# Turning the normalised tokens of an attention and expert layer: eight TensorE turns a group, or VectorE turns of 32 x 32 squares with SBUF exchanges

## What is computed

```python
# first layer, on layernorm(x)
g = jax.nn.sigmoid(jnp.einsum('bld,ed->ble', x, Wg) + bg)
h[l] = (1 - g[l]) * h[l-1] + g[l] * x[l]          # associative scan over l
attn = jnp.einsum('bld,ed->ble', h, Wo) + bo
x = x + layernorm(attn)
# second layer, on layernorm(x), E = 8 experts, C = 320, H = 1024
probs = jax.nn.softmax(xf @ router_w + router_b); eid = argmax(probs)
rank = position of the token among those of its expert; valid = rank < C
y_tok = relu(x @ w1[eid] + b1[eid]) @ w2[eid] + b2[eid]      # where valid
yov   = relu(xf @ ow1 + ob1) @ ow2 + ob2                      # otherwise
x = x + layernorm(where(valid, y_tok, yov))
```

## Time and profile before

| | us |
|---|---|
| median of 3 runs | 1164.59 (1164.39 to 1166.16) |
| the profiled execution | 1166.17 |
| its span in the profile | 1163.0 |

### The profile page before, as it was taken

The page is one execution under the profiler, slowest core; times in us unless marked ns, Lnnn a source line. Parts: engine busy times, 40 slices in busy tenths (PEclk is TensorE's granted clock), DMA queues, the critical chain, the costliest instruction groups (busy, mean ns, idle before and its releaser), DMA issues.

```text
span 1163.0 us, 24424 instructions
## 1 busy us (share of the span) xinstructions
PE 1142.6 (98%) x7549; PEld 1020.4 (88%) x7549; DVE 991.5 (85%) x2741; ACT 742.1 (64%) x1375; POOL 690.1 (59%) x792
## 2 busy tenths in 40 slices
PE   8999999999999999999999999999999999999996
PEld 4788898888988898888888888988898888899996
DVE  6888988888888988989898888888888987688885
ACT  4366666666656666666666666656666666678782
POOL 3556567675656666565657665656666664414444
PEclk9999999999999999999999999999999999999998
DMA  9121110100111111111101101111111100335430
GB/s 262 58 100 56 55 46 35 43 27 30 36 36 36 36 36 36 36 36 36 36 19 35 34 23 33 36 36 36 36 36 36 36 18 20 114 114 191 145 130 34
DMA packets 59428, 65.09 MB, mean 56 GB/s; under 512 B 7835, under 2 KB 55629, under 8 KB 59268
## 3 DMA queue, kind: packets, MB, share of 16 engines
q1 hardware_dynamic: 52228, 59.36, 15.8%
q0 software_dynamic: 7168, 5.34, 1.5%
HBM read 40.19 MB, written 38.76 MB: 68 GB/s over the span
## 4 chain that ended last, share of the span: by engine, by line
PE 90%; DVE 5%; POOL 2%; ACT 1%; issue 1%; DMA 0%; DVEq 0%; POOLq 0%; ACTq 0%
PE psY L1430 12%; PE psY L1433 11%; PE psY L1432 11%; PE psH L1324 11%; PE psH L1325 11%; PE psH L1326 10%; PE psA L1324 5%; PE psA L1325 5%; PE psA L1326 5%; PE psT L1380 3%; PE psT L1337 2%; DVE st L859 1%; PE psT L1393 1%; PE psT L1395 1%; PE psA L1498 1%
## 5 line engine op out<-in xcount | busy, mean ns | idle before, releaser
L621 ACT ACTIVATE hid<-psH,biasT 128x512 f32<-128x512 f32 (+1 forms) x312 | 202.9, 650 | 217.6 <-PE psH L1326 215.2
L1430 PE MATMUL psY<-W_hi,hid_hi 128*128 128x256 f32 x1168 | 336.1, 288 | 0.6 <-DVE hid_lo L1012 0.5
L1433 PE MATMUL psY<-W_hi,hid_lo 128*128 128x256 f32 x1168 | 330.3, 283 | 0.0
L1432 PE MATMUL psY<-W_lo,hid_hi 128*128 128x256 f32 x1168 | 330.2, 283 | 0.0
L399 POOL TENSOR_TENSOR rstd<-veps,mhalf 128x4 f32<-128x4 f32 (+2 forms) x103 | 141.4, 1373 | 163.2 <-DVE nmean L871 163.2
L1012 DVE TENSOR_TENSOR hid_lo<-hid,hid_hi 128x512 fp32r<-128x512 f32 (+1 forms) x308 | 200.6, 663 | 42.5 <-ACT hid_hi L626 35.8
L1324 PE MATMUL psH<-xfT_hi,W_hi 128*128 128x512 f32 (+1 forms) x624 | 235.9, 378 | 0.3 <-ACT hid L621 0.2
L1325 PE MATMUL psH<-xfT_lo,W_hi 128*128 128x512 f32 (+1 forms) x624 | 234.9, 376 | 0.0
L1326 PE MATMUL psH<-xfT_hi,W_lo 128*128 128x512 f32 (+1 forms) x624 | 232.7, 373 | 0.0
L1430 PEld LDWEIGHTS psY<-W_hi,hid_hi 128*128 128x128 f32 x1168 | 222.7, 191 | 9.9 <-DVE hid_lo L1012 1.6
L1432 PEld LDWEIGHTS psY<-W_lo,hid_hi 128*128 128x128 f32 x1168 | 223.0, 191 | 5.9
(11 more groups left out here) (173 smaller groups left out, 2176.8 us busy)
## 6 DMA issues: line engine op xcount, KB each, us to landing
xin<-L_attn_x SPq DMA_DIRECT2D x32, 512.0 KB, 3.4
stage<-L_ffn_w SPq DMA_DIRECT2D x16, 1024.0 KB, 5.2
out<-outt SPq DMA_DIRECT2D x31, 512.0 KB, 2.8
xbuf<-zrow SPq DMA_DIRECT2D x1, 2590.0 KB, 16.5
xin<-xbuf SPq DMA_DIRECT2D x8, 259.0 KB, 4.9
stage<-L_ffn_ow SPq DMA_DIRECT2D x2, 1024.0 KB, 8.5
xbuf<-x,idx POOLq DMA_INDIRECT x128, 2.1
b_b<-L_ffn_b SPq DMA_DIRECT2D x1, 1024.0 KB, 6.5
```

The lines of the kernel that those rows point to most:

```text
L621: act.activation(hid[j % 2][:, at:n], psH[:, j % 2, at:n], ACT.Relu, bias=bias).then_inc(s_hid, 1)
L1430: pe.matmul(dst, hi, w[0][:, j, :], start=(j == 0 and (tail or t % 2 == 0)), stop=False, skip_group_check=True)
L1432: pe.matmul(dst, hi, w[1][:, j, :], start=False, stop=False, skip_group_check=True)
L1433: last = pe.matmul(dst, lo_, w[0][:, j, :], start=False, stop=(j == HC - 1), skip_group_check=True)
```

## The change

From group 6 on (`PIPED`) the tokens are turned without TensorE. For such a group:

- x is loaded a second time, a step earlier, into `x_ahead`, the first half of stage (`load_ahead`); statistics and norm0 read it there. xin is still loaded for residual1.
- VectorE's stats0 handles group g+4 instead of g+3, as one piece ahead of lo(7); before, the moments stood behind xf_lo.
- GpSimd's norm0 handles g+3 instead of g+2, in the same place of the step. Before it writes tok it waits until the blocks of the group before have landed.
- SP exchanges tok into `tok_blocks[v]` (the second half of stage) with 16 DMAs of 32 partitions each, SBUF to SBUF, behind the load of x (`exchange_blocks`). A DMA moves the square (b, a) of each 128x128 tile to (a, b), in runs of 32 elements (128 bytes).
- VectorE turns each 32 x 32 square of tok_blocks into psT with two `transpose` instructions of 128x512, between stats1 and residual2 (`turn_blocks`).
- TensorE leaves out transposes0 in those steps (26 of them).
- The first expert's weights are loaded in the steps 28 and 29 instead of step 1, since stage is in use until then. Steps 2 and 3 are written out instead of looped, and the last four steps of GpSimd.

The diff, cut to its core:

```diff
+SQ = 32
+PIPED = 6
...
+def piped(g):
+    return not isinstance(g[0], int) or 2 * g[0] + g[1] >= PIPED
...
+        tok_blocks = [stage[:, 1, v * TG * D:(v + 1) * TG * D].rearrange("p (t d) -> p t d", d=D) for v in range(2)]
+        x_ahead = stage[:, 0, 0:TG * D].rearrange("p (t d) -> p t d", d=D)
+
+        def xin_of(g):
+            return x_ahead if piped(g) else xin[g[1]]
...
+            def load_ahead(g):
+                i, v = g
+                if piped(grp(i, v, -1)):
+                    sp.wait_ge(s_tok, cnt(g, 1, 0))
+                sp.sem_inc(s_held_sp, 1)
+                sp.dma_start(x_ahead, x[i, v * GT:(v + 1) * GT, :].rearrange("(t p) d -> p t d", p=P))\
+                    .then_inc(s_x_ahead[v], 16)
+
+            def exchange_blocks(g):
+
+                i, v = g
+                src = tok[:].rearrange("p t d -> p (t d)").rearrange("p (n c) -> p n c", c=P)
+                dst = tok_blocks[v].rearrange("p t d -> p (t d)").rearrange("p (n c) -> p n c", c=P)
+                sp.wait_ge(s_tok, cnt(g, 1, 1))
+                sp.sem_inc(s_held_sp, 1)
+                sp.wait_ge(s_T0, cnt(grp(i, v, -1), 2, 0))
+                sp.sem_inc(s_held_sp, 1)
+                for a in range(P // SQ):
+                    for b in range(P // SQ):
+                        sp.dma_start(dst[a * SQ:(a + 1) * SQ, :, b * SQ:(b + 1) * SQ],
+                                     src[b * SQ:(b + 1) * SQ, :, a * SQ:(a + 1) * SQ]).then_inc(s_blocks[v], 16)
...
-                prev, nxt, far = grp(i, u, -1), grp(i, u, 1), grp(i, u, 3)
+                prev, nxt, far, beyond = grp(i, u, -1), grp(i, u, 1), grp(i, u, 3), grp(i, u, 4)
+                if piped(beyond) and live(beyond, NG):
+                    load_ahead(beyond)
                 if live(prev, NG):
                     store(prev)
                 if live(far, NG):
                     sp.wait_ge(s_x1, cnt(nxt, 1, 1))
                     load(far)
+                    if piped(far):
+                        exchange_blocks(far)
...
-                pool.wait_ge(s_T0, cnt(g, 2, 0))
+                before = grp(i, v, -1)
+                if piped(before):
+                    pool.wait_ge(s_blocks[before[1]], landed((before[0] - PIPED // 2, before[1]), (P // SQ) ** 2))
+                else:
+                    pool.wait_ge(s_T0, cnt(g, 2, 0))
                 pool.sem_inc(s_held, 1)
                 for t in range(TG):
-                    last = pool.tensor_scalar(tok[:, t, :], xin[v][:, t, :], rstd[0][:, t:t + 1], nmr[0][:, t:t + 1],
+                    last = pool.tensor_scalar(tok[:, t, :], xin_of(g)[:, t, :], rstd[0][:, t:t + 1], nmr[0][:, t:t + 1],
...
-                if live(far, NG):
+                if not piped(far):
                     norm0(far)
+                elif live(beyond, NG):
+                    norm0(beyond)
                 if live(nxt, NG):
                     deviation(1, nxt, TG)
+                    if piped(beyond) and not piped(far):
+                        norm0(beyond)
...
+            def turn_blocks(g):
+                i, v = g
+                dve.wait_ge(s_blocks[v], landed((i - PIPED // 2, v), (P // SQ) ** 2))
+                for c in range(DC):
+                    dve.transpose(psT[:, c, :], tok_blocks[v][:, :, c * P:(c + 1) * P]).then_inc(s_T0, 1)
...
+                if piped(grp(i, u, 3)) and not piped(far):
+                    stats0(grp(i, u, 3))
...
                     stats1(nxt)
+                if ahead and piped(far):
+                    turn_blocks(far)
                 if live(grp(i, u, -1), NG):
                     residual2(grp(i, u, -1))
...
-                next_x = grp(i, u, 3)
+                next_x = grp(i, u, 4 if piped(grp(i, u, 3)) else 3)
                 if live(next_x, NG):
-                    read_rows0(next_x)
+                    stats0(next_x)
                 low(7)
                 if up:
                     xf_lo(nxt, GT)
-                if live(next_x, NG):
-                    moments(0, next_x, TG)
...
-                    if j == 3 and ahead:
+                    if j == 3 and ahead and not piped(far):
                         transposes0(far)
```

More of the change, by code:

```diff
@@ L210, in sandwich_kernel @@
         s_T0 = sem("s_T0")
+        s_blocks = sems("s_blocks")
+        s_x_ahead = sems("s_x_ahead")
+        s_held_sp = sem("s_held_sp")
         s_xn_hi = sem("s_xn_hi")
@@ L327, in _ @@
             sp.wait_ge(s_l2, HC)
-            load_w1((0, 0))
-            load_w2((0, 0))
             step(0, 1)
-            with sp.Fori(1, NG // 2 - 2) as i:
+            for u in range(2):
+                step(1, u)
+            with sp.Fori(2, NG // 2 - 2) as i:
                 for u in range(2):
                     step(i, u)
-            for u in range(4):
-                step(*grp(NG // 2 - 2, u, 0))
+            step(NG // 2 - 2, 0)
+            sp.wait_ge(s_tok, NG)
+            load_w1((0, 0))
+            step(NG // 2 - 2, 1)
+            sp.wait_ge(s_T0, 2 * NG)
+            load_w2((0, 0))
+            for u in range(2):
+                step(NG // 2 - 1, u)
             def load_rows(e):
@@ L465, in step @@
                 prev, now, nxt, far = grp(i, u, -1), grp(i, u, 0), grp(i, u, 1), grp(i, u, 2)
+                beyond = grp(i, u, 3)
                 if live(prev, NG):
                     deviation(3, prev, TG, t0=sure(prev))
-                if live(far, NG):
+                if not piped(far):
                     norm0(far)
+                elif live(beyond, NG):
+                    norm0(beyond)
                 if live(nxt, NG):
                     deviation(1, nxt, TG)
+                    if piped(beyond) and not piped(far):
+                        norm0(beyond)
                     renumber(nxt)
@@ L515, in _ @@
             second_step((0, 0), (0, 1), (1, 0), (1, 1))
-            with pool.Fori(1, NG // 2 - 1) as i:
+            for u in range(2):
+                step(1, u)
+            with pool.Fori(2, NG // 2 - 2) as i:
                 for u in range(2):
                     step(i, u)
-            for u in range(2):
-                step(NG // 2 - 1, u)
+            for u in range(4):
+                step(*grp(NG // 2 - 2, u, 0))
             def keep_rows(e):
@@ L880, in read_rows0 @@
                 i, v = g
-                dve.wait_ge(s_x_in[v], landed(g))
-                read_rows(0, lambda t: xin[v][:, t, :], TG)
+                if piped(g):
+                    dve.wait_ge(s_x_ahead[v], landed((i - PIPED // 2, v)))
+                else:
+                    dve.wait_ge(s_x_in[v], landed(g))
+                read_rows(0, lambda t: xin_of(g)[:, t, :], TG)
             def stats0(g):
@@ L1252, in _ @@
             second_step(*(grp(0, 0, k) for k in range(5)))
-            with dve.Fori(1, NG // 2 - 2) as i:
+            for u in range(2):
+                step(1, u)
+            with dve.Fori(2, NG // 2 - 2) as i:
                 for u in range(2):
@@ L1595, in _ @@
             second_step(A, B, (1, 0), (1, 1))
-            with pe.Fori(1, NG // 2 - 1) as i:
+            for u in range(2):
+                step(1, u)
+            with pe.Fori(2, NG // 2 - 1) as i:
                 for u in range(2):
```

## The result

In its first measurement the changed kernel takes **1188.5 us** (median of 4 runs, 1187.6 to 1189.2), the kernel before 1164.5 (1164.2 to 1166.2): ratio 1.0199, 95% interval 1.0186 to 1.0212. It is 24 us slower where 3.9 us less were forecast, and 0.5 us above the range. The profiled execution took 1188.88 us, 1187.1 of them span. The same kernel, not a character changed, took 1181.7 us in a second measurement and **1159.7 us** in a third (e13, ratio 0.9952, 0.9936 to 0.9969), while the medians of the kernel before lay between 1164.3 and 1165.4 in every measurement.

A forecast was written before the change was run, and what follows sets the result against it. TensorE, busy 98%, was taken to set a 31.17 us step; VectorE's and GpSimd's loops would then limit it to 31.02, saving 26 x 0.15 = 3.9 us from 1164.59, giving 1160.7 us. The range was 1150 to 1188.

The forecast's parts named there:

- VectorE starts its result as soon as layer2(7) ends, so this closes a loop: At the step's end: lo(7) delayed to 29.42, next step starts at 31.00 us, so VectorE paces the step.
- 0.26 us late already: Before layer2(2): VectorE's lo(2) ends at 14.16 us of the step, where TensorE, 0.90 early, wants it at 13.90.
- limits of 31.00 and 31.04 us: Step lengths set by VectorE's loop and by GpSimd's through tok2; they fall together, and 31.02 was taken.
- The turn: Between stats1 and residual2 on VectorE: two 128x512 transposes at 0.70 us each, 1.40 for both.
- The fourth rival: On VectorE: the turn costs as much as the scan, 2.42 us; step 32.0, +22 us, 1187 us. Chance 15%.
- The estimate from the Trainium skill's figure: For VectorE's 128x512 turn: 0.73 us, from the skill's 311 ns for a 128x128 bf16 turn.
- TensorE's matmuls: At transposes0 (L1337): 26 x 8 = 208 matmuls go, 0.90 us a step less on TensorE.
- GpSimd's loop: From stats2's nmean: tok2 at 27.23 us makes transposes1 wait, step 31.04; hst_lo at 34.91 makes project 0.4 late.
- VectorE's loop: Turn 1.40 and moments 0.68 us, less idle time, put lo(7) at 29.42; the step is 31.00 us.
- Full gain: The turn hides in VectorE's spare time, so TensorE's 26 x 0.90 = 23 us come whole: 1141 us. Chance 7%.
- Held moments: Moments ahead of lo(7) caught behind a GpSimd instruction: 0.5 us a step, +9 us, 1173 us. Chance 26%.
- Late blocks: Exchanged blocks land after GpSimd's norm0 needs them, 38.6 us after step start: 1180 up to 1300 us. Chance 8%.

The follow-up runs named there:

- e13: The changed kernel once more, unaltered, in its third measurement: 1159.7 us, ratio 0.9952 to the kernel before.
- session A: The first measurement of the changed kernel, beside the kernel before (a session is kernels measured together on one chip, one after the other): 1188.5 us.
- e8: The kernel before with one line moved: the moments of the next x ahead of lo(7) instead of behind xf_lo. 1164.1 us, ratio 0.9997.
- e11: The changed kernel with neither exchange nor turn on VectorE: TensorE transposes again, moments still ahead of lo(7); a repeat of e2, unaltered. 1165.8 us.
- e10: The changed kernel without the 16 exchange transfers: GpSimd writes into the block buffers, VectorE turns the unexchanged squares, values wrong. 1164.9 us here, 1160.1 us when first measured.
- e9: The changed kernel once more, unaltered, in its second measurement: 1181.7 us.
- e17: The changed kernel with the 16 transfers in runs of 1 KB, squares not exchanged; a repeat of e14, unaltered. 1187.0 us.
- e7: The changed kernel with the same 4096 runs of 128 B in 4 transfers instead of 16, moving columns within a partition, squares not exchanged. 1175.3 us.
- e5: The changed kernel with the exchange issued early, right behind the load of x a step ahead and ahead of the store. 1176.5 us.
- e6: The changed kernel with the four row scatters of a step left out, an element-wise GpSimd instruction in place of each. 1158.5 us.
- e3: The changed kernel with the exchange kept but no turn on VectorE; TensorE transposes its result, values wrong. 1165.5 us.
- session B: The group of experiments measured together that holds e2, e3 and two others, without late signals and without a copy of the changed kernel.
- e16: The changed kernel with both the exchange early (as e5) and GpSimd's hst_lo ahead of the scatters (as e12). 1159.1 us.
- e12: The changed kernel with GpSimd's hst_lo ahead of the four row scatters instead of behind them. 1171.0 us.
- sessions A, C, D and F: Sessions with late signals: A is the first measurement, C holds e5, e6, e7 and e8, D holds e9, e10, e11 and e12, F holds e17 and one other.
- e14: The changed kernel with the 16 transfers in 1 KB runs instead of 128 B, squares not exchanged; a repeat of an earlier run, unaltered. 1159.7 us.
- e2: The changed kernel with neither exchange nor turn on VectorE: TensorE transposes the block buffers, moments still ahead of lo(7). 1165.7 us.

## Why the prediction was wrong

**The step that failed** is the sentence "VectorE starts its result as soon as layer2(7) ends, so this closes a loop". In session A it starts 2.10 us after, mean of the steps. No term of the sum and none of the rivals had TensorE's signal itself arriving late, and the trace of before holds no case of it: all its increments came 0.01 to 0.02 us after their matmul. Of the 2.06 us more, 1.11 reach the step (32.06 against 30.95), and 26 x 1.11 = 29 us is the whole distance between the two measurements of one kernel, 1188.5 - 1159.7. Most of the other 0.95 falls into waits that were there. VectorE's wait for hid_hi shrinks by 0.4 us a step, and the `veps` behind `result`, which in e13 is held until GpSimd's hst_lo ends (at 499.98), takes 0.17 in session A, 0.4 less. First e13 and then the changed kernel in session A, each with its `veps` and with its waits over 13 steps:

```profile
499.44 0.58 DVE L928 TENSOR_SCALAR veps<-mv 128x4 f32<-128x4 f32 x1
...
DVE ysb L1095 <- PE psY L1506: 11.2, 13, 0.9
...
DVE hid_lo L1081 <- ACT hid_hi L684: 6.9, 13, 0.6
...
PE psA L1397 <- POOL hst_lo L512: 5.3, 13, 0.4
```

```profile
514.01 0.17 DVE L928 TENSOR_SCALAR veps<-mv 128x4 f32<-128x4 f32 x1
...
DVE ysb L1095 <- remote: 38.1, 13, 3.0
...
PE psY L1503 <- DVE hid_lo L1081: 6.1, 12, 0.8
PE psA L1397 <- POOL hst_lo L512: 5.3, 13, 0.4
...
DVE hid_lo L1081 <- ACT hid_hi L684: 1.6, 6, 0.3
```

and TensorE, which never waited for hid_lo in the window of e13, waits for it 6.1 us in session A, before layer2(2): the place where the prediction had VectorE 0.26 us late already.

**Why the kernel before doesn't show it.** In sessions with late signals e8 and e11, which keep the turns on TensorE, have `result` 0.46 and 0.44 us late in the mean and lose nothing (1164.1 and 1165.8); of the kernel before itself there are only times from these sessions, medians of 1164.3 to 1165.4. TensorE set their pace and VectorE had 2.4 to 4.7 us to spare. The change spends that margin: it takes 0.90 us from the engine that paced the step and puts the work on the one that must answer every signal.

It also moves the scatters against that signal. The last scatter of a step, in session A, where layer2(7) ends at 508.46, and in e8, where it ends at 497.04 (timelines of GpSimd):

```profile
508.88 0.97 POOL L472 DMA_INDIRECT xbuf<-x,idx  x1 [0.30 <-issue]
```

```profile
496.04 0.98 POOL L421 DMA_INDIRECT xbuf<-x,idx  x1 [0.31 <-issue]
```

By the record of packets the last scatter's end 0.75 us after layer2(7) in that step of e8 and 0.2 us before it in the steps between, where `result` is on time; in the changed kernel and in e10 they end about 2.15 us after it in every step. (In the trace of the kernel before, which has no late signal, they end 1.45 us after it and 0.15 before it in turn.) So `result` can be late by some 2.2 us in every step, where in e8 it was late by 1.0 in every other one; and in the mean it is 0.46 us late without the exchange (e10) and 1.87 with it (e9).

The forecast counted 3.9 us of gain and had limits of 31.00 and 31.04 us that "fall together", which is another way to say that no margin was left; it should have asked what an added us at each of VectorE's waits would cost, and would have found up to 26 us for each, on the slower side only.

**The sum, term by term**, against e13. The turn: 0.70 each was taken, and the 52 rows have 702 ns at the median (682 to 727), 1.31 the pair, where 1.40 was taken. The fourth rival (as slow as the scan) is refuted, though its time, 1187, is what session A measured: a time alone would have named the wrong cause. The estimate from the Trainium skill's figure (VectorE: DVE Perf Modes, The three transpose paths) was 0.73, 4% above the rows. TensorE's matmuls: minus 208, right. GpSimd's loop: 31.04 was computed and 30.95 measured, and this loop is the bound, but by its other arm. The 31.04 is tok2's at transposes1, for which TensorE doesn't wait in e13; it waits 0.42 for hst_lo at project, where 0.4 was said, and the prediction had put that wait inside TensorE's slack. VectorE's loop: 31.00 was too long, since VectorE waits 0.84 us for layer2(7) before `result`, and TensorE doesn't wait for lo(7) either. Total: 1160.7 against 1159.7, in part by luck, since neither of the two limits that gave the sum was there.

**The rivals.** Full gain: no, for the reason given, GpSimd. Held moments: `veps` behind the moments of x takes 0.17, and e8 puts the price of the order at nothing. Late blocks: the issues take 10.44 us for 16 (0.61 each at the median where 0.5 was taken) and end 29.3 us after S, and the last landing on record is at 30.6, against 38.6 needed; GpSimd never waits for a transfer. VectorE is busy 27.9 of 30.95 us, 90% and not over 92%.

**What stays open.** What makes a session one with late signals. Why the exchange makes them later there: runs of 1 KB don't cure it (e17), a quarter of the completions doesn't either (e7 against e5), nor does an exchange that has landed some 9 us before the signal (e5); whether an early one is better than one beside the scatters isn't settled, since 1176.5 and 1188.5 or 1181.7 are from different sessions. e6 shows that the scatters are needed, not how they hold a signal. The exchange beside TensorE's turns (e3) was measured in session B alone, so what it would cost there in a session with late signals is open. The late increments are known from one trace per kernel; whether they are there without the profiler is not shown.

No complete version here beats the kernel before in both kinds of session. In a session without late signals all that turn on VectorE are 0.4 to 0.5% faster, e16 most (1159.1); with them the kernel before and those with TensorE's turns and no exchange (e8, e11) stay at 1164 to 1166, and the others take 1165 (e10, whose values are wrong) to 1188.5.

## What to carry to other kernels

An edit that moves work from the pacing engine to one that answers its signals is paid twice: in time, which rows tell, and in margin, which they tell only if you ask for it; price a late us at each wait of the loop that becomes the bound, and if several limits fall within a tenth of a us, give the slower side more than the sum does. Ask also what work of the other engines the edit moves beside the signal that becomes critical. Measure the kernel under test again in every session that holds an experiment on it: session B, clean and without it, made me believe in a cause that copies of it then refuted. Where a wait's releaser is named "remote" or "issue" on one core, compare the matmul's end with the recorded increment before looking for another engine.

## What the runs showed of the hardware

A 128x512 fp32 turn of 32 by 32 squares on VectorE, from SBUF into PSUM, takes 702 ns, within 3% of the element-wise instructions of that size (685 ns).

Signals of TensorE can arrive late while TensorE itself runs on. At 508.46 in session A layer2(7) was done, layer1(0) of the next step followed without a gap, and the increment came 2.15 us later, 0.08 us ahead of layer1(0)'s. This lay beside GpSimd's indirect row scatters, moved with them (e12), was gone without them (e6), and came in sessions A, C, D and F for every kernel that scatters: 568 of 569 late increments belong to matmuls that ended beside a step's scatters. In those sessions the record also lacks about half of the scatters' own increments (26 to 35 of 64 a step held, where the other sessions hold 60 to 64).

4096 runs of 128 B between SBUF partitions, 512 KB in 16 transfers, are as cheap for the rest of the core as 512 runs of 1 KB in a session without late signals: 1159.7 us both (e13, e14). Where TensorE turns, the kernel takes 1165.5 with them and 1165.7 without (e3, e2). SP issues one in 0.61 us.
